# Attention sums: tiles 8 to 15 added by accumulating DMAs, four partial sums joined on GpSimd

## What is computed

```python
q = concat(q_c, q_r); k = concat(k_c, k_r)          # 8 heads, 128 + 32 columns
scores = einsum('bhsd,bhtd->bhst', q, k) / sqrt(160)
attn = softmax(scores, axis=-1)
o = einsum('bhst,bhtd->bhsd', attn, v_c)
x = x + o.reshape(b, s, 8 * 128) @ W_O + b_O
```

## Time and profile before

| | |
|---|---|
| median of 3 runs | 737.66 us (737.27 to 738.73) |
| profiled execution, span | 737.8 us |
| TensorE matmul busy | 718.6 us, 97% |
| VectorE busy | 629.4 us, 85% |
| ScalarE busy | 466.1 us, 63% |
| GpSimd busy | 583.5 us, 79% |
| first attention's blocks | about 38 to 491 us |

### The profile page before, as it was taken

One profiled execution on the slowest core, in us unless ns is written; L12 is line 12 of the kernel. 1 busy time (PEld: TensorE's weight loads), 2 busy tenths in 40 slices (PEclk: granted clock), 3 DMA queues, 4 the chain that ended last, 5 costly groups with the idle time before them and its releaser, 6 DMA issues.

```text
span 737.8 us, 12518 instructions
## 1 busy us (share of the span) xinstructions
PE 718.6 (97%) x4180; PEld 469.0 (64%) x4180; DVE 629.4 (85%) x1304; ACT 466.1 (63%) x1069; POOL 583.5 (79%) x484
## 2 busy tenths in 40 slices
PE   8999999999999999999999999999899999999997
PEld 7665655655656656556556555466666699778885
DVE  8889999999999999999999899765978736878885
ACT  4367766766767767767667676654777831455553
POOL 6489989999999999999989999963689861446774
PEclk9999999999999999999999999999999999999999
DMA  6300000000000000000000000012000000032431
GB/s 148 91 1 2 1 2 2 2 3 2 1 2 2 1 2 3 1 1 2 2 1 3 2 1 2 2 46 74 2 1 0 2 1 1 1 87 74 141 103 28
DMA packets 40679, 15.57 MB, mean 21 GB/s; under 512 B 27292, under 2 KB 36525, under 8 KB 40616
## 3 DMA queue, kind: packets, MB, share of 16 engines
q1 hardware_dynamic: 39336, 14.67, 8.2%
q10 hardware_dynamic: 1280, 0.12, 0.1%
HBM read 13.35 MB, written 1.10 MB: 20 GB/s over the span
## 4 chain that ended last, share of the span: by engine, by line
PE 74%; POOL 11%; issue 7%; DVE 6%; ACT 1%; DMA 0%; POOLq 0%; DVEq 0%
PE ps L1482 17%; PE ps L1468 16%; PE ps L1526 15%; POOL hid_lo L1007 5%; PE ps L1510 4%; PE ps L1880 4%; PE ps L1537 3%; POOL nrm L987 2%; DVE mx L1061 2%; PE ps L1920 2%; PE ps L1922 1%; PE ps L1921 1%; POOL hid L987 1%; PE ps L1455 1%; PE ps L1456 1%
## 5 line engine op out<-in xcount | busy, mean ns | idle before, releaser
L1061 DVE TENSOR_REDUCE mx<-ps 128x1 f32<-128x512 f32 x492 | 302.6, 681 | 14.7 <-PE ps L1468 13.2
L622 ACT ACTIVATE prob<-ps 128x512 f32<-128x512 f32 x512 | 262.7, 630 | 9.2 <-PE ps L1482 9.1
L1482 PE MATMUL ps<-q_cols,key 128*128 128x512 f32 x512 | 209.5, 412 | 0.8 <-ACT prob L622 0.8
L1468 PE MATMUL ps<-key,q_rows 128*128 128x512 f32 x512 | 204.7, 404 | 0.8 <-DVE key L1047 0.4
L901 POOL TENSOR_TENSOR part<-part,prob 128x512 f32<-128x512 f32 x124 | 158.6, 1290 | 30.4 <-DVE part L1076 25.9
L1482 PEld LDWEIGHTS ps<-q_cols,key 128*128 128x128 f32 x512 | 95.4, 187 | 89.5 <-issue 50.7
L1526 PE MATMUL ps<-prob,val 128*32 128x512 f32 x1024 | 124.1, 598 | 0.0
L1468 PEld LDWEIGHTS ps<-key,q_rows 128*128 128x128 f32 x512 | 95.6, 188 | 23.0 <-DVE mx L1061 5.5
L901 POOL TENSOR_TENSOR part<-part,pair 128x512 f32<-128x512 f32 x64 | 95.9, 1499 | 0.1
L1007 POOL TENSOR_TENSOR hid_lo<-hid,hid_hi 128x512 fp32r<-128x512 f32 x44 | 61.5, 1410 | 38.6 <-ACT hid_hi L785 38.6
L901 POOL TENSOR_TENSOR pair<-prob 128x512 f32<-128x512 f32 x64 | 82.7, 1293 | 1.9 <-ACT prob L622 1.8
(11 more groups left out here) (285 smaller groups left out, 1172.6 us busy)
## 6 DMA issues: line engine op xcount, KB each, us to landing
g_all<-g_rows SPq DMA_DIRECT2D x9, 256.0 KB, 3.3
den<-den_sb SPq DMA_DIRECT2D x124, 2.0 KB, 2.1
g_all<-g_rows SPq DMA_DIRECT2D x6, 224.0 KB, 3.0
X<-in_L_attn_h_t_dram SPq DMA_DIRECT2D x4, 256.0 KB, 4.5
out_dram<-X SPq DMA_DIRECT2D x4, 256.0 KB, 2.4
g_all<-g_rows SPq DMA_DIRECT2D x6, 128.0 KB, 3.1
g_all<-g_rows SPq DMA_DIRECT2D x4, 192.0 KB, 3.6
w_raw<-in_L_ffn_w_g_dram SPq DMA_DIRECT2D x1, 704.0 KB, 4.5
```

The lines of the kernel that those rows point to most:

```text
L622: act.activation(prob[:, g % RING, :], ps[:, g % 3, :], ACT.Exp, scale=SCALE).then_inc(s_exp, 1)
L1061: dve.tensor_reduce(mx[:, n % 2, c % TPB, at:at + 1], ps[:, BANK["rows", 2 * lin + j], :], AX.X, ALU.max).then_inc(s_mrd, 1)
L1468: pe.matmul(ps[:, BANK["rows", 2 * lin + j], :], q_rows[:, k, i * P:(i + 1) * P], key[:, h % KBUF, c0:c0 + BLK], start=True, stop=True).th ...
L1482: pe.matmul(ps[:, g % 3, :], key[:, n // NB % KBUF, t * P:(t + 1) * P], q_cols[:, n % NB, :], start=True, stop=True).then_inc(s_sc, 1)
```

## The change

Of a block's 16 tiles GpSimd now adds only 0 to 7, in two instructions of 128x1024 (`begin_sums`: sums 0 and 1 get tiles 0+4 and 1+5, sums 2 and 3 get 2+6 and 3+7). Tiles 8 to 11 and tiles 12 to 15 are added to the four sums by two DMAs issued from GpSimd's queue with an adding operation (`late_sums`), 128 partitions x 2048 elements each; `s_late` counts them. Later GpSimd adds the four sums into one (`join_parts`), in two instructions, of 1024 and of 512 elements. VectorE's `begin_sum` and `dsum` are gone. ScalarE's exponential waits at tile 0 for `begin_sums` of the block before, at tile 8 for its first DMA and at tile 12 for its second. `totals` multiplies 4 x 128 columns in place of 4 x 512, two blocks behind and in slot 1; the denominators' DMAs move 128 words each; `output` and `accumulate` move from slot 1 to slot 6. The last but one block is not joined, its `totals` adds the four sums in TensorE, in slot 4 of the last block.

```diff
@@ -189,8 +189,8 @@
         NW = NT // (2 * NG)
-        VSUM = (2, 3)
-        ADDS = NT - NG - len(VSUM)
+        LATE = 2
+        MANY = NBLK - 2
         LEAD = CPB + 2
@@ -198,12 +198,10 @@
-        pair = sb("pair", [P, 2, BLK])
-        den = sb("den", [P, 2, NG, TPB])
+        den = sb("den", [P, 2, TPB])
-        dsum = sb("dsum", [P, 2, TPB])
@@ -211,6 +209,15 @@
         s_sc, s_exp, s_pv, s_sum = sem("s_sc"), sem("s_exp"), sem("s_pv"), sem("s_sum")
+        s_late = sem("s_late")
+        def begun(n):
+            return 2 if n == 0 else 4 * n + 2 if n < NBLK - 1 else 4 * n
+        def joined(n):
+            return 4 * n + 5
         s_usb, s_ops, s_rden, s_acc = sem("s_usb"), sem("s_ops"), sem("s_rden"), sem("s_acc")
@@ -218,8 +225,7 @@
-        def SUMS_AT(n):
-            return 6 if n < NBLK - 2 else 4
+        SUMS_AT, OUT_AT = 1, 6
@@ -239,18 +245,16 @@
                     todo += [("folded", 0), ("folded", 1)]
-                if slot == 1 and 2 <= n < NBLK - 1:
+                if slot == SUMS_AT and 2 <= n < NBLK - 1:
+                    todo.append(("sums", n - 2))
+                if slot == OUT_AT and 2 <= n < NBLK - 1:
                     todo.append(("out", n - 2))
-                if slot == SUMS_AT(n) and 1 <= n < NBLK - 1:
-                    todo.append(("sums", n - 1))
-                if slot == 7 and n == NBLK - 2:
-                    todo.append(("out", n - 1))
             for item in todo:
-        for item, bank in ((("sums", NBLK - 1), 6), (("norm", 0), 3), (("sums", NBLK - 2), 5), (("out", NBLK - 2), 5), (("norm", 1), 4),
-                           (("out", NBLK - 1), 5)):
+        for item, bank in ((("sums", NBLK - 3), 4), (("out", NBLK - 3), 6), (("sums", NBLK - 2), 5), (("norm", 0), 3),
+                           (("out", NBLK - 2), 5), (("sums", NBLK - 1), 6), (("norm", 1), 4), (("out", NBLK - 1), 5)):
             place_item(item, bank)
@@ -471,10 +475,11 @@
                     if n >= 2:
-                        sp.wait_ge(s_rden, 2 * (n - 1))
-                    with nc.allow_non_contiguous_dma("4 x 128 x 4 words"):
+                        sp.wait_ge(s_rden, n - 1)
+                    with nc.allow_non_contiguous_dma("4 x 32 x 4 words"):
                         for g in range(NG):
-                            sp.dma_start(den[:, n % 2, g, :], den_sb[C * g:C * g + 1, :].rearrange("a (p i) -> a p i", i=TPB)).then_inc(s_dend, 16)
+                            sp.dma_start(den[C * g:C * (g + 1), n % 2, :],
+                                         den_sb[C * g:C * g + 1, 0:P].rearrange("a (p i) -> a p i", i=TPB)).then_inc(s_dend, 16)
@@ -605,7 +610,7 @@
-                        act.copy(den_sb[:, :], ps[:, BANK["sums", n], :]).then_inc(s_densb, 1)
+                        act.copy(den_sb[:, 0:P], ps[:, BANK["sums", n], 0:P]).then_inc(s_densb, 1)
@@ -615,10 +620,12 @@
                         act.wait_ge(s_pv, NW * (n - 1) + 1)
-                        act.wait_ge(s_sum, ADDS * (n - 1) + 5)
-                    elif g >= RING and t == NT // 2:
+                        act.wait_ge(s_sum, begun(n - 1))
+                    elif g >= RING and t == 2 * NG:
                         act.wait_ge(s_pv, NW * n)
-                        act.wait_ge(s_sum, ADDS * n)
+                        act.wait_ge(s_late, 16 * (LATE * (n - 1) + 1))
+                    elif g >= RING and t == 3 * NG:
+                        act.wait_ge(s_late, 16 * LATE * n)
                     act.activation(prob[:, g % RING, :], ps[:, g % 3, :], ACT.Exp, scale=SCALE).then_inc(s_exp, 1)
@@ -650,7 +657,9 @@
                             sums(n - 1)
-                        if t == (2 * SUMS_AT(n) + 2 if n < NBLK - 1 else 8) and n >= 1:
+                        if t == 2 * SUMS_AT + 2 and n >= 2:
+                            sums_out(n - 2)
+                        if t == 10 and n == NBLK - 1:
                             sums_out(n - 1)
@@ -890,70 +899,53 @@
+                def tiles(n, first, count):
+                    at = (NT * n + first) % RING
+                    return prob[:, at:at + count, :]
                 def ready(n, tile):
-                def first_sums(n):
...
+                def begin_sums(n, j):
+                    if n >= 2 and j == 0:
                         pool.wait_ge(s_ones, n - 1)
+                    ready(n, NG + 2 * j + 1)
+                    pool.tensor_tensor(part[:, n % 2, 2 * j:2 * j + 2, :], tiles(n, 2 * j, 2), tiles(n, NG + 2 * j, 2), ALU.add).then_inc(s_sum, 1)
+                def late_sums(n, j):
+                    ready(n, NG * (j + 3) - 1)
+                    if j == 0:
+                        pool.wait_ge(s_sum, begun(n))
+                    else:
+                        pool.wait_ge(s_late, 16 * (LATE * n + j))
+                    pool.dma_start(part[:, n % 2, :, :], tiles(n, NG * (j + 2), NG), accum_op=ALU.add).then_inc(s_late, 16)
+                def join_parts(n):
+                    pool.wait_ge(s_late, 16 * LATE * (n + 1))
+                    p = part[:, n % 2, :, :]
+                    pool.tensor_tensor(p[:, 0:2, :], p[:, 0:2, :], p[:, 2:4, :], ALU.add).then_inc(s_sum, 1)
+                    pool.wait_ge(s_sum, joined(n) - 1)
+                    pool.tensor_tensor(p[:, 0, :], p[:, 0, :], p[:, 1, :], ALU.add).then_inc(s_sum, 1)
+                for n in range(NBLK):
+                    begin_sums(n, 0)
                     if n < 2:
                         columns(n + 2)
...
-                def last_sums(n):
...
-                    pool.wait_ge(s_sumd, len(VSUM) * n + 1)
-                    ready(n, 10)
-                    add(total[2], total[2], tile(10))
...
-                for n in range(NBLK - 1):
-                    first_sums(n)
-                    last_sums(n)
+                    if 1 <= n < NBLK - 1:
+                        join_parts(n - 1)
+                    begin_sums(n, 1)
+                    if n < NBLK - 1:
+                        late_sums(n, 0)
+                        late_sums(n, 1)
                     if n == NBLK - 2:
                         ln0_pool(pool, 0)
-                        ln0_pool(pool, 1)
-                first_sums(NBLK - 1)
-                summed(NBLK - 1, 5)
-                add(part[:, 1, 1, :], part[:, 1, 1, :], pair[:, 1, :])
                 pool.memset(anchors2[:, :], 0.0).then_inc(s_aside, 1)
+                ln0_pool(pool, 1)
                 ln0_pool(pool, 2)
@@ -1068,13 +1060,6 @@
-                def begin_sum(n, g):
-                    t = NT * n + NG * g
-                    if n >= 2:
-                        dve.wait_ge(s_ones, n - 1)
-                    dve.wait_ge(s_exp, t + 2)
-                    dve.tensor_tensor(part[:, n % 2, g, :], prob[:, t % RING, :], prob[:, (t + 1) % RING, :], ALU.add).then_inc(s_sumd, 1)
                 def key_biases(m, bank):
@@ -1091,12 +1076,10 @@
                         dve.wait_ge(s_dend, 16 * NG * (n + 1))
-                        dve.tensor_reduce(dsum[:, n % 2, :], den[:, n % 2, :, :].rearrange("p g i -> p i g"), AX.X, ALU.add).then_inc(s_rden, 1)
-                        dve.wait_ge(s_rden, 2 * n + 1)
-                        dve.reciprocal(rden[:, n % 2, :], dsum[:, n % 2, :]).then_inc(s_rden, 1)
+                        dve.reciprocal(rden[:, n % 2, :], den[:, n % 2, :]).then_inc(s_rden, 1)
                     else:
                         dve.wait_ge(s_den_ps, 1)
-                        dve.reciprocal(rden[:, n % 2, :], ps[:, BANK["sums", n], 0:TPB]).then_inc(s_rden, 2)
+                        dve.reciprocal(rden[:, n % 2, :], ps[:, BANK["sums", n], 0:TPB]).then_inc(s_rden, 1)
@@ -1159,25 +1142,23 @@
                                 queries_lo(n + 2, BANK["queries", n + 2])
-                        if slot == 1 and 2 <= n < NBLK - 1:
-                            denominators(n - 2)
-                            accumulate(n - 2)
                         if slot == 2 and n == 0:
                             minus_max(n + 1)
-                            begin_sum(n, VSUM[0])
-                        if slot == 6 and n < NBLK - 1:
-                            begin_sum(n, VSUM[1])
+                        if slot == OUT_AT and 2 <= n < NBLK - 1:
+                            denominators(n - 2)
+                            accumulate(n - 2)
                         if n == NBLK - 2 and slot == 7:
                             ln0_stats(dve, 0)
-                            denominators(n - 1)
-                            accumulate(n - 1)
-                            ln0_stats(dve, 1)
                         if n == NBLK - 1:
                             elif slot == 3:
+                                denominators(n - 2)
+                                accumulate(n - 2)
+                                ln0_stats(dve, 1)
+                            elif slot == 5:
                                 ln0_norm(dve, 1)
@@ -1532,9 +1513,16 @@
                     bank_read(("sums", n))
```

(58 more changed lines are left out.)

16 lines of the change are left out of this document (2 added, 14 removed).

## The result

| | before | after |
|---|---|---|
| median | 737.47 us | 978.0 us (977.34 to 978.75) |
| profiled span | 737.8 us | 975.6 us |
| ratio to before | | 1.326, 95% interval 1.324 to 1.328 |
| TensorE / VectorE / GpSimd busy | 97% / 85% / 79% | 80% / 61% / 50% |
| granted TensorE clock, mean | 0.996 | 0.918 |

What follows compares the result with a forecast made beforehand. GpSimd's queue with its accumulating DMAs was taken as the bound, 2 x 6.7 + 6.0 = 19.4 us a round for 30 rounds; with start and end, 491.2 + 62 D = 907 us, range 745 to 1100.

Steps and rivals of the forecast that it cites:

- closed loop D + J + B + D: GpSimd's in-order queue: two DMAs, join and one begin in series, 19.4 us a round against 13.9 a block before.
- J and B: GpSimd's join (1024 and 512 elements) and one begin_sums addition (1024): 6.0 us together with waits, 5.1 to 6.6.
- D: Time from issue to landing of one 1 MB accumulating DMA: 6.7 us taken, within 5.9 to 8.7.
- the sum: Whole kernel: 231.1 + 62 D + 260.1 = 907 us.
- Start and end: First DMA issued at 51.1 us; from totals(30) in block 31 to the kernel's end 260.1 us, as before.
- Where the others wait: ScalarE's tiles in each round: about 1 us idle ahead of tile 8 and 5 us ahead of tile 12.
- The clock: TensorE's granted clock falls behind gaps, losing 1.7 us once a round, at no cost on the loop.
- What the change takes away: Per block: totals falls from 0.86 to 0.2 to 0.4 us on TensorE; VectorE loses 1.7 us of additions and dsum.
- GpSimd's busy share: GpSimd idle twice a block, its busy share down from 79% to some 45% of the span.
- The plain price: Accumulating DMA costs no more than a plain copy, landing in 3.9 to 5.3 us: 776 us (733 to 820); chance 0.20.
- The fast side: Landing under 3.65 us hides the DMAs; TensorE alone bounds at 13.3 us a block: 720 us; chance 0.07.
- The slower rival: Accumulating DMA dearer than two reads, through GpSimd's descriptors or slow adding; landing 10 us gives 1111 us; chance 0.15.

Runs made afterwards that it cites:

- quarter DMA: The changed kernel with each accumulating DMA moving one tile (256 KB) into sum 0, six of eight late tiles left out of the denominators: 747.9 us.
- run of 736.4 us: Changed kernel with one accumulating DMA a block (tiles 12 to 15), sums redivided between VectorE and GpSimd, join behind its issue, output and accumulate in slot 7: 736.4 us.

## Point by point: where the prediction was right and where not

- **The bound.** Right: a closed loop D + J + B + D on GpSimd's queue, and no engine's work in it but GpSimd's additions. Taking the join out (102 of 111 us) and moving it (213 us) both show it.
- **J and B.** Right: 2.37 + 1.28 + 2.32 us and two hand-overs of 0.07 are 6.1, where 6.0 was forecast.
- **D.** The right mechanism, 0.3 us too low: 7.0 us to landing where 6.7 was taken. At 62 us of time for each microsecond that is 19 us.
- **The hand-over to the DMA.** Missing from the sum: the DMA instruction starts 0.5 us after its wait is met, where an addition starts after 0.07 at most. Twice a round and 30 rounds make some 30 us. This was no question of D: the sum took D from issue to landing and had nothing for the time from a met wait to the issue.
- **Late landings.** Missing too. The mean round is 21.7 us: 23 of them take 21.0 to 21.8 and seven 22.6 to 23.4. The median landing is 7.0 us and the mean 7.24, which twice a round is the 0.5 us. The three terms together (0.6 + 1.0 + 0.5, with 0.2 of hand-overs) turn 19.4 into 21.7 us, and 30 x 2.3 = 69 us is what the forecast fell short of the span, 975.6 us. 50 of these 69 us are terms that the sum did not have, so with D exactly right it would have said 925.
- **Start and end.** Right: first DMA at 51.22 (51.1 forecast), `totals(30)` at 717.28 and 258.3 us from there to the end (260.1 forecast).
- **Where the others wait.** Half right. Ahead of tile 12 ScalarE waits 4.5 to 7.5 us, mostly 5.3 to 5.6 (5 forecast), ahead of tile 8 1.4 us in some rounds and nothing in most (1 forecast). Missed: 4.1 us ahead of tile 0, 30 times, where ScalarE waits for begin_sums(n-1,1), which stands behind the join. The prediction had let ScalarE run from tile 12 to tile 7 without that wait. It cost nothing, as the loop ends last.
- **The clock.** It fell as forecast, to 0.918 on the mean and 0.79 in the window behind a wait, partly at the 1.2 GHz level. That it costs nothing agrees with the chain of the round shown, in which no TensorE piece stands; no run tests it.
- **What the change takes away.** Right in size and worth nothing here: `totals` is 0.22 us in the chain where it is read in the run with the join moved, 0.86 before; VectorE's two additions and `dsum` are gone.
- **GpSimd's busy share.** 50%, not 45: the DMA instruction counts 0.88 us, 55 us in all.
- **Rivals.** The plain price (776 us, chance 0.20) falls with the landing of 7.0 us; a copy that does have it, at 4.6 us, gave 824 us. The fast side (720 us) was to begin at D under 3.65 us. The quarter DMA has 3.2 us and came out at 748 us, with rounds of 14.2 us, so that edge was too high: with the 0.5 us to issue put in twice it lies at (13.3 - 7.0) / 2 = 3.15 us, an estimate from this case's rows. The slower rival (1111 us) is not far from the truth in one thing, the 0.5 us to issue, but the bytes explain all of the landing.

The landing of one DMA was bounded from rows of other DMAs only, and the time hung on it 62 times; the range was wide for that reason. The choice of 6.7 us within 5.9 to 8.7 had only an argument behind it, and that it came within 0.3 us is in part luck.

## What to carry to other kernels

Before a step is moved from an engine to a DMA, write down what of it is awaited in turn: two DMAs that must follow each other cost their full landing time in series, whatever the engines' shares say, and here the place of one call in GpSimd's queue was worth 213 us. Price an accumulating DMA inside SBUF over 128 partitions as these runs had it, at 1.9 us plus 1.28 us for each 256 KB, about twice what a plain copy's bytes take, and add half a microsecond for GpSimd to start it. When two engines are close to full, shift their additions against each other and look at the durations of both before adding or removing work on either. A nearly full engine need not be the bound: GpSimd went from 12.8 to 10.5 us a block here for 0.35 us more on TensorE, and the block became 0.25 us longer.

## What the hardware showed that was not expected

- **A DMA instruction of GpSimd starts 0.5 us after its wait is met**; the chain above has 0.47 and 0.50 us as "issue" ahead of it, and 0.07 ahead of an addition.
- **The large DMAs that land late have an instruction fetch among their packets.** The DMA queues' rows for two windows of the changed kernel, from the issue of a first DMA to that of the second, one of 9.1 us and one of 7.4:

```profile
q0 software_dynamic: 144, 1.05, 56.4%
q1 hardware_dynamic: 184, 0.00, 1.0%
q8 instruction: 1, 0.02, 0.6%
...
part<-prob POOLq DMA_DIRECT2D x1, 1024.0 KB, 8.6
```

```profile
q0 software_dynamic: 144, 1.05, 68.9%
q1 hardware_dynamic: 144, 0.00, 1.2%
q14 instruction: 1, 0.01, 0.5%
...
part<-prob POOLq DMA_DIRECT2D x1, 1024.0 KB, 6.9
```

  The packet of q8 is 16 KB of instructions; the 8 KB packet of the other instruction queue, q14, in the second window did not make that DMA late. By the trace's packet records 13 of the changed kernel's 62 DMAs have a q8 packet among theirs, and from first to last packet they took 5.5 to 6.7 us; the other 49 took 5.1 to 5.3. The run without the join has 14 such DMAs with 5.2 to 6.9 us, and 48 others with up to 5.6. The run of 736.4 us has 7 with 5.2 to 7.0 and 24 others with up to 5.9. So in these three runs every DMA over 6 us has such a packet, and some that have one are not late. Which of the two causes the other is not shown: in 9 of the 13 the packet of q8 begins 5.5 us or more after the DMA's first, later than the 5.1 to 5.3 us in which the other 49 were through. No run takes the fetches away.
- **Small DMAs of another queue take longer beside large ones.** `nmx` to `q_cols`, 2 KB from SP's queue, had 1.9 us before and has 4.6 on the median in the changed kernel, where 30 of the 32 are in flight together with an accumulating DMA; in the run of 736.4 us only one of them is, and the median is 1.9 again.
- **Two additions on VectorE and GpSimd that read SBUF lock each other out.** VectorE's 1.2 us become 3.2 to 3.5, or GpSimd's first 2.4 become 3.4. The one that starts second pays, and 0.02 to 0.2 us decide which that is.
